# Sorting a graph's edges in 32 steps of 26 columns, with the sums cleared in parts

## The chip, the cores and the metric

The kernel runs on one core of one Trainium2 chip. The metric is the device time of one execution in microseconds (us): the median of three runs of the kernel before is 2950.52 us (2949.51 to 2952.47).

TensorE (PE in the profile) multiplies, VectorE (DVE), ScalarE (ACT) and GpSimd (POOL) work on whole tiles, and SyncE (SP) issues DMAs. DMAs whose addresses come from a table, gathers and scatters, are issued by POOL.

## The reference

A graph layer on 6250 nodes of 256 features and 106250 edges (two directions of 50000 random pairs and one loop per node), then a mixture of six experts, of which each node takes two:

```
deg        = segment_sum(ones, row); denom = maximum(deg, 1)
neigh_sum  = segment_sum(X[col], row)              # X is the layer norm of x
H          = relu(X @ W_root + (neigh_sum / denom) @ W_neigh + b)
gg         = segment_sum(abs(H[row] - H[col])**2, row) / denom
x          = x + tanh(gg)
x          = x + experts(layernorm(x))             # router, top 2 of 6, three layers each
```

Both segment sums go over all edges, so the kernel first brings the edges into the order of their target blocks, on the chip.

## The kernel before, in words

**Stages.** (1) The edges are read, each gets a place by its target's block of 128 nodes (49 blocks), and a table of places is made; this ends some 111 us into the span. (2) The edge sort, which the change touches. (3) The sorted lists are read back and turned into indices (`idx`) and rows within a block (`local`). (4) Pass 1 over the edges: for each of 842 tiles of 128 edges POOL gathers 128 rows of `xn_table`, DVE makes a hot matrix, PE multiplies, DVE adds the product to one block of `acc`. (5) h is made from the sums, (6) pass 2 does the same with `h_table`, (7) the experts.

**The edge sort.** The edges stand in 832 columns (`TW`) of 128. They are taken in 16 chunks (`CC`) of 52 columns (`TH`), and a chunk in steps of `BT` columns; before, `BT` is 13, which is four steps a chunk and 64 in all. In a step `k`, with `c` the chunk and `t` the step in it:

- DVE (`dve_edges`) makes `is_col` (L956: 64 numbers of each column), `hot_lane` (L960: 128 numbers of each), and `hot_col` (L964, two instructions: the first half of it for the columns that ACT leaves over, the second half for all). All are 16-bit products or comparisons of two tiles in SBUF.
- ACT (`act_edges`) makes the first half of `hot_col` for the first `BY_ACT` columns (L776), one instruction for each column.
- PE (`pe_edges`) multiplies `hot_lane` and `hot_col` column by column into one sum per chunk (L692), once all of the step's three parts are there.

`is_col`, `hot_lane` and `hot_col` have two slots each, so step `k` waits until step `k - 2` was used. When a chunk's sum is complete ACT copies its low part (`act_low`, L820), DVE puts low and high together into `lists` (`dve_list`, L1090, with one operand in PSUM), and POOL issues four scatters of the list to `edge_list` in DRAM (L630), each by 128 addresses from `dest`. For the first eight chunks DVE also marks rows (`dve_passed`, L1084), PE sums them (`pe_rows`, L740), and DVE makes the addresses (`dve_rows`, L1098 and L1101, both with an operand in PSUM).

**The product rows beside it.** From step `Z_AT` on, PE makes after each step's products one block of product rows (`pe_z`, L730), and ACT scales it into `z_rows` (`act_z`, L810) one step later. `z_rows` has 8 slots. SP writes four blocks at a time to `xn_table` (`sp_nodes`, L1108); ACT waits for such a write before it overwrites its slots. PE's instructions for the next step stand behind `pe_z`.

**Clearing.** `acc` shares its memory (`big`) with the sort's tiles: columns 0 to `sorting_end` are in use until the sort ends. The rest is cleared while the sort runs, by one DMA that repeats `local`, still zero, 20 times (L534, L536), issued by SP ahead of the writes of product rows. The part below `sorting_end`, 7814 columns, is cleared by DVE (L1175) behind the indices.

What orders the work is the order in which each engine's function issues it; nothing rearranges it. Each engine runs its instructions in that order and waits for semaphores in front of them. The lines of the sort are these:

## Time and profile before

| | |
|---|---|
| median of 3 runs | 2950.52 us |
| span of the profiled execution | 2957.2 us, 32069 instructions |
| PE busy | 2373.3 us (80%) |
| DVE busy | 2010.2 us (68%) |
| ACT busy | 855.2 us (29%) |
| POOL busy | 2030.6 us (69%) |

The profile is of one further execution, whose span from the first to the last instruction is 2957.2 us; the page has no other time of it. Shares over the whole span say little of the sort, which is some 185 us of it. How to read the rows: a scatter or gather on POOL is busy while POOL makes its descriptors; the data land later. Spans of matmuls are modelled, and an instruction of DVE or ACT that follows another closely is shown as starting shortly before the former ends.

### The profile page before, as it was taken

The page shows a single profiled execution, that of the slowest core. Times are in us where ns is not written, and L with a number is a line of the kernel's source. Part 1 is how long each engine was busy: PE and PEld are TensorE (multiplying, and loading weights), DVE is VectorE, ACT ScalarE, POOL GpSimd, SP SyncE. Part 2 cuts the span into 40 slices and gives each one's busy share as a digit, 9 for nine tenths or more (in the row PEclk, how much of TensorE's full clock was granted, in tenths as well). Part 3 has the DMA queues.
Part 4 walks back from the last instruction along what each step waited for, and adds up shares of the span by engine and source line. Part 5 has one row for each costly group of instructions (what it writes and reads, how often), then busy time and mean ns, then how long its engine had stood idle before and what let it go on. Part 6 is the DMA issues. An engine that isn't in the chain of part 4 may idle for free.

```text
span 2957.2 us, 32069 instructions
## 1 busy us (share of the span) xinstructions
PE 2373.3 (80%) x8745; PEld 1336.0 (45%) x8745; DVE 2010.2 (68%) x5189; ACT 855.2 (29%) x2372; POOL 2030.6 (69%) x2062
## 2 busy tenths in 40 slices
PE   6676677777777777773988998889899997899993
PEld 4554444444444444341333333333333333788993
DVE  8997655555555555556777777777777778556654
ACT  7887000000000000003333333333333334455551
POOL 2488777777777777777777777777777772323666
PEclk8597777777777777876999999999999998999997
DMA  3443333333333333335433333333333334333555
GB/s 123 170 98 46 103 106 105 105 105 105 106 105 105 105 105 105 105 105 170 142 105 112 105 105 105 105 105 105 105 105 105 105 105 148 102 122 95 156 152 154
DMA packets 172773, 334.43 MB, mean 113 GB/s; under 512 B 42912, under 2 KB 108428, under 8 KB 172338
## 3 DMA queue, kind: packets, MB, share of 16 engines
q0 software_dynamic: 100176, 249.03, 29.6%
q1 hardware_dynamic: 72418, 83.34, 8.6%
q8 instruction: 72, 1.18, 0.2%
q14 instruction: 107, 0.88, 0.1%
HBM read 281.12 MB, written 41.88 MB: 109 GB/s over the span
## 4 chain that ended last, share of the span: by engine, by line
PE 35%; DVE 19%; DMA 16%; POOL 12%; issue 11%; DVEq 5%; ACT 2%; SPq 0%; POOLq 0%; ACTq 0%
PE ps L1271 22%; DVE big L1312 11%; POOL arena L1237 10%; DMA arena<-xn_table,graph 8%; PE ps L2083 7%; DMA arena<-h_table,graph 4%; DVEq L1281 4%; PE ps L2057 3%; DVE graph L1306 2%; DVE late L1352 1%; ACT big L776 1%; DVE big L964 1%; PE ps L2035 1%; DMA big<-y_table,node 1%; PE ps L1322 1%
## 5 line engine op out<-in xcount | busy, mean ns | idle before, releaser
L1271 PE MATMUL ps<-arena,graph 128*128 128x258 f32 (+3 forms) x3956 | 1706.5, 600 | 398.9 <-DVE graph L1306 388.2
L1271 PEld LDWEIGHTS ps<-arena,graph 128*128 128x128 f32 (+1 forms) x3956 | 773.3, 226 | 1316.0 <-DVE graph L1306 1095.0
L1312 DVE TENSOR_TENSOR big<-ps,big 128x258 f32 (+1 forms) x1978 | 1099.4, 556 | 135.3 <-PE ps L1271 102.0
L1237 POOL DMA_INDIRECT arena<-xn_table,graph x842 | 798.3, 948 | 261.3 <-issue 193.2
L1237 POOL DMA_INDIRECT arena<-h_table,graph x842 | 798.8, 949 | 258.0 <-issue 136.4
L1306 DVE TENSOR_SCALAR graph<-iota,graph 128x128 f32<-128x128 f32 x1684 | 502.1, 298 | 570.6 <-DMA arena<-xn_table,graph 353.9
L1250 ACT ACTIVATE arena<-arena 128x256 f32<-128x256 f32 x842 | 349.4, 416 | 706.6 <-DMA arena<-h_table,graph 706.3
L1368 ACT ACTIVATE node<-late 128x256 f32<-128x256 f32 x49 | 19.7, 413 | 1044.6 <-DVE late L1352 1044.0
L1655 POOL DMA_INDIRECT arena<-xn_table,node x113 | 116.7, 1033 | 211.8 <-PE ps L2035 121.6
L630 POOL DMA_INDIRECT edge_list<-big x64 | 136.2, 2128 | 45.8 <-issue 45.5
L2083 PE MATMUL ps<-arena 128*128 128x128 f32 x904 | 122.2, 279 | 16.3 <-issue 13.6
L776 ACT ACTIVATE big<-arena,big 128x64 f16<-128x64 f16 x512 | 129.7, 363 | 11.7 <-DVE arena L956 11.5
L1704 DVE TENSOR_TENSOR big<-ps,node 128x256 f32<-128x256 f32 x113 | 47.8, 423 | 119.5 <-PE ps L2057 119.2
L1667 POOL DMA_INDIRECT big<-y_table,node x98 | 101.7, 1038 | 33.3 <-issue 23.7
L2083 PE MATMUL ps<-big,arena 128*128 128x128 f32 x904 | 121.8, 279 | 0.0
L2083 PEld LDWEIGHTS ps<-arena 128*128 128x128 f32 x904 | 111.0, 193 | 20.2 <-issue 17.2
L2057 PE MATMUL ps<-node,big 128*128 x452 | 117.8, 384 | 0.8 <-DVE big L1704 0.8
L2083 PEld LDWEIGHTS ps<-big,arena 128*128 128x128 f32 x904 | 112.4, 196 | 0.3 <-issue 0.3
L692 PE MATMUL ps<-big,arena 128*128 128x128 f16 x832 | 69.0, 242 | 46.1 <-ACT big L776 29.2
L1695 DVE COPY arena<-node 128x1028 f32 x113 | 81.8, 725 | 22.2 <-issue 9.3
L692 PEld LDWEIGHTS ps<-big,arena 128*128 128x128 f16 x832 | 58.5, 109 | 67.2 <-issue 53.0
L1974 ACT ACTIVATE big<-ps,arena 128x128 f32<-128x128 f32 x226 | 70.7, 365 | 58.1 <-PE ps L2083 55.7
(319 smaller groups left out, 1596.1 us busy)
## 6 DMA issues: line engine op xcount, KB each, us to landing
y_table<-big SPq DMA_DIRECT2D x55, 256.0 KB, 2.5
arena<-xn_table,graph POOLq DMA_INDIRECT x842, 2.8
arena<-h_table,graph POOLq DMA_INDIRECT x842, 2.7
big<-graph SPq DMA_DIRECT2D x1, 8480.0 KB, 46.5
xn_table<-late SPq DMA_DIRECT2D x12, 512.0 KB
late<-h_table SPq DMA_DIRECT2D x12, 512.0 KB, 4.7
xn_table<-big SPq DMA_DIRECT2D x12, 512.0 KB, 4.6
result<-big SPq DMA_DIRECT2D x12, 512.0 KB
```

Of the source, the lines that this page charges most:

```text
L630: e.indirect_dma_start(out=edge_list[c % 2], out_offset=bass.IndirectOffsetOnAxis(ap=dest[:, c, g:g + 1], axis=0), in_=lists[:, c, g * R8: ...
L692: m = e.matmul(ps[4 + c % 2][:, 0:2 * HI], hot_lane[:, r, u, :], hot_col[:, r, u, :, :].rearrange("p a m -> p (a m)"), start=(t == 0 and u ...
L776: e.activation(hot_col[:, r, u, 0, :], is_col[:, r, u, :], ACT.Copy, scale=code_f[:, t0 + u:t0 + u + 1]).then_inc(s_hcola, 1)
L1237: e.indirect_dma_start(out=row, out_offset=None, in_=table, in_offset=bass.IndirectOffsetOnAxis(ap=idx[:, t:t + 1], axis=0)).then_inc(s_ro ...
L1250: e.activation(rows2[:, sq, :], rows2[:, slot, :], ACT.Square).then_inc(s_sq, 1)
L1271: e.matmul(out_, hot[part, g % HOTS, :], moving, start=True, stop=True).then_inc(s_sum[i], 1)
L1281: _, places = nc.values_load_multi_w_load_instructions(offs[0:1, a:z], engines=[mybir.EngineType.DVE], min_val=0, max_val=(NB - 1) * W2, s ...
L1306: e.tensor_scalar(hot[:, g % HOTS, :], iota[:, :], local[:, t:t + 1], None, ALU.is_equal).then_inc(s_hot[i], 1)
L1312: e.tensor_tensor(block, ps[a % BANKS][:, 0:width], block, ALU.add)._wait_ge(s_sum[i], a + 1).then_inc(s_add[i], 1)
L1655: e.indirect_dma_start(out=xg[:, k % XR, :], out_offset=None, in_=xn_table, in_offset=bass.IndirectOffsetOnAxis(ap=tok[:, k:k + 1], axis=0 ...
L2057: m = e.matmul(ps[3][:, 0:D], h2[:, n % 2, j * P:(j + 1) * P], records_flat[:, bass.ds(place + (W12 + j * D), D)], start=(j == 0), stop=(j ...
L2083: t = e.matmul(bank[:, m * P:(m + 1) * P], wbuf[:, k % WR, at_:at_ + P], moving[:, j * P:(j + 1) * P], start=(j == 0), stop=(j == KD - 1))
```

## The change

A step takes 26 columns, so a chunk has two steps and the sort has 32. `BY_ACT` doubles with it: ACT still makes 16 of 26 columns as it made 8 of 13. `hot_lane` no longer fits into one place and its two slots lie apart, one in `arena` and one in `big`; `hot_col` doubles too. So `sorting_end` grows from 7814 to 11142.

Product rows start at step 3 in place of 6, and two blocks are made a step in place of one. ACT now scales the first of the two after its ninth activation of the next step (`u == BY_ACT // 2`), behind `act_low` where there is one, and the second after its sixteenth. `pe_rows` stands ahead of the waits of its step, `dve_rows` moves to the first step of the next chunk, `dve_list` to the second step, and the variance block `dve_variance` from step 3 to step 1.

The one clearing DMA is cut into 13 parts (`sp_clear`) of one or two repetitions of `local`, each issued by SP behind one write of product rows, 16 repetitions in all. Of the columns below `sorting_end` DVE clears 7002, and ACT the 4140 above them, in nine activations behind its last `act_low`. The semaphore `s_unit` is folded into `s_nrow`.

The diff, without changes of assertions and names:

```diff
-    BT = 13
+    BT = 26
-    Z_AT, ZR = 6, 8
+    Z_AT, ZR, ZS = 3, 8, 2
-    BY_ACT = 8
+    BY_ACT = 16
...
-        hot_lane = arena[:, 0:BT * P].bitcast(F16).rearrange("p (r t m) -> p r t m", r=2, t=BT)
...
+        clear_at = max(codes_at + 2 * NT, codes_at + TW)
+        hot_lane = [a.bitcast(F16).rearrange("p (t m) -> p t m", t=BT)
+                    for a in (arena[:, 0:BT * P // 2], carve_sort(BT * P // 2))]
         sorting_end = at
...
             e.wait_ge(s_pick, NB)
-            times, over = divmod(NB * W2 - sorting_end, NTR)
-            e.dma_start(acc[:, sorting_end:NB * W2 - over].rearrange("p (n w) -> p n w", w=NTR),
-                        local.unsqueeze(1).to_broadcast([P, times, NTR])).then_inc(s_cleared, 16)
-            e.dma_start(acc[:, NB * W2 - over:NB * W2], local[:, 0:over]).then_inc(s_cleared, 16)
+
+        times, over = divmod(NB * W2 - sorting_end, NTR)
+        clear_cut = [times * i // len(z_sets) for i in range(len(z_sets) + 1)]
+        clear_parts = [i for i in range(len(z_sets)) if clear_cut[i + 1] > clear_cut[i]]
+
+        def sp_clear(e, i):
+            n = clear_cut[i + 1] - clear_cut[i]
+            at_ = sorting_end + clear_cut[i] * NTR
+            e.dma_start(acc[:, at_:at_ + n * NTR].rearrange("p (n w) -> p n w", w=NTR),
+                        local.unsqueeze(1).to_broadcast([P, n, NTR])).then_inc(s_cleared, 16)
+            if i == clear_parts[0]:
+                e.dma_start(acc[:, NB * W2 - over:NB * W2], local[:, 0:over]).then_inc(s_cleared, 16)
...
                 c, t = divmod(k, TH // BT)
                 r = k % 2
+                if t == 1 and c < C:
+                    pe_rows(e, c)
                 e.wait_ge(s_hlane, k + 1)
...
                 m.then_inc(s_sorted, 1)
-                if t == 1 and c < C:
-                    pe_rows(e, c)
-                if Z_AT <= k < Z_AT + NB:
-                    pe_z(e, k - Z_AT)
+                for b in z_at(k - Z_AT):
+                    pe_z(e, b)
...
+        def z_at(i):
+
+            return range(ZS * i, min(ZS * i + ZS, NB)) if i >= 0 else range(0)
...
+                made_before = z_at(k - Z_AT - 1)
                 for u in range(BY_ACT):
                     e.activation(hot_col[:, r, u, 0, :], is_col[:, r, u, :], ACT.Copy,
                                  scale=code_f[:, t0 + u:t0 + u + 1]).then_inc(s_hcola, 1)
-                if t == 1 and c:
-                    act_low(e, c - 1)
-                if 0 < k - Z_AT <= NB:
-                    act_z(e, k - Z_AT - 1)
+                    if u == BY_ACT // 2:
+                        if t == 1 and c:
+                            act_low(e, c - 1)
+                        for b in made_before[0:1]:
+                            act_z(e, b)
+                for b in made_before[1:]:
+                    act_z(e, b)
             act_low(e, CC - 1)
+            blank = sorting_end - clear_at
+            for a in range(0, blank, 4 * P):
+                n = min(4 * P, blank - a)
+                e.activation(acc[:, clear_at + a:clear_at + a + n],
+                             ones[:, 0:1].to_broadcast([P, n]), ACT.Copy, scale=0.0).then_inc(s_blank, 1)
...
+                if t == 0 and 0 < c <= C:
+                    dve_rows(e, c - 1)
                 if t == 0 and c < C:
                     dve_passed(e, c)
-                if t == 2 and c:
+                if t == 1 and c:
                     dve_list(e, c - 1)
-                if t == 3 and c < C:
-                    dve_rows(e, c)
-                if k == 3:
+                if k == 1:
                     dve_variance(e)
...
                             z_rows[:, b0 % ZR:b0 % ZR + n, :]).then_inc(s_zout[i % 2], 16)
+                if i in clear_parts:
+                    sp_clear(e, i)
...
-            e.wait_ge(s_cleared, 32)
+            e.wait_ge(s_cleared, 16 * (len(clear_parts) + 1))
...
-            e.memset(acc[:, 0:sorting_end], 0.0).then_inc(s_one, 1)
+            e.memset(acc[:, 0:clear_at], 0.0).then_inc(s_one, 1)
+            e.wait_ge(s_blank, -(-(sorting_end - clear_at) // (4 * P)))
```

In the changed kernel every line below the functions that grew has a higher number: `is_col` is L980, `hot_lane` L984, `hot_col` L988, `dve_list` L1114, ACT's part of `hot_col` L792, `act_low` L844, `act_z` L834.

On DVE, one chunk of the later half, from behind one list (L1090) to the next, stood so before:

```order
L956 TENSOR_TENSOR arena<-graph,arena 128x832
L960 TENSOR_TENSOR arena<-graph,arena 128x1664
L964 TENSOR_TENSOR big<-arena 128x5x64
L964 TENSOR_TENSOR big<-arena 128x13x64
L1090 SCALAR_TENSOR_TENSOR big<-ps,big 128x64
```

The first four rows come four times before the next L1090; the list of a chunk comes behind the third step of the next one. Now the same stretch of DVE reads:

```order
L980 TENSOR_TENSOR arena<-graph,arena 128x1664
L984 TENSOR_TENSOR big<-graph,arena 128x3328
L988 TENSOR_TENSOR big<-arena 128x10x64
L988 TENSOR_TENSOR big<-arena 128x26x64
L1114 SCALAR_TENSOR_TENSOR big<-ps,big 128x64
```

The four come twice between two lists, with twice the columns each, and the list stands behind the second of them.

On ACT, while product rows are made, a step was eight activations and one block of product rows:

```order
L776 ACTIVATE big<-arena,big 128x64 x8
L820 ACTIVATE big<-ps 128x64
L810 ACTIVATE late<-ps,rstd 128x256
L776 ACTIVATE big<-arena,big 128x64 x8
L810 ACTIVATE late<-ps,rstd 128x256
```

Now two steps on ACT read as follows, the step with a chunk's low part first:

```order
L792 ACTIVATE big<-arena,big 128x64 x9
L844 ACTIVATE big<-ps 128x64
L834 ACTIVATE late<-ps,rstd 128x256
L792 ACTIVATE big<-arena,big 128x64 x7
L834 ACTIVATE late<-ps,rstd 128x256
L792 ACTIVATE big<-arena,big 128x64 x9
L834 ACTIVATE late<-ps,rstd 128x256
L792 ACTIVATE big<-arena,big 128x64 x7
L834 ACTIVATE late<-ps,rstd 128x256
```

Of each pair of blocks the first now stands between the ninth and the tenth activation of the step that follows its product, ahead of seven activations that PE needs.

## Rows read from the trace of the kernel before

**Rows 1.** Chain that ended last, in order of time: start us, us, what
```profile
144.54 18.86 DMA xn_table<-late
...
289.94 2.88 DMA edge_list<-big
```

**Rows 2.** The page's costliest groups: line, engine, operation, count | busy, mean ns | idle before
```profile
L1237 POOL DMA_INDIRECT arena<-xn_table,graph x842 | 798.3, 948 | 261.3 <-issue 193.2
```

**Rows 3.** Groups by form, 111.4 to 277 us: count | busy us, mean ns | idle before
```profile
L776 ACT ACTIVATE big<-arena,big 128x64 f16<-128x64 f16 x512 | 129.7, 363 | 11.7 <-DVE arena L956 11.5
L630 POOL DMA_INDIRECT edge_list<-big x57 | 125.4, 2199 | 43.6 <-issue 43.3 <-DMA edge_list<-big 0.3
...
L960 DVE TENSOR_TENSOR arena<-graph,arena 128x1664 f16<-128x1664 f16 x64 | 65.1, 1018 | 1.7 <-PE ps L692 1.4
...
L956 DVE TENSOR_TENSOR arena<-graph,arena 128x832 f16<-128x832 f16 x64 | 37.3, 583 | 5.4 <-ACT big L776 5.4
L964 DVE TENSOR_TENSOR big<-arena 128x832 f16<-128x832 f16 x64 | 37.3, 583 | 0.0
...
L964 DVE TENSOR_TENSOR big<-arena 128x320 f16<-128x320 f16 x64 | 20.3, 317 | 0.0
```

**Rows 4.** Timeline, one step in chunk 8: start us, us, engine, line, what [idle before]
```profile
212.07 2.03 ACT L776 ACTIVATE big<-arena,big 128x64 f16<-128x64 f16 x8
...
213.22 0.58 DVE L956 TENSOR_TENSOR arena<-graph,arena 128x832 f16<-128x832 f16 x1
213.72 1.01 DVE L960 TENSOR_TENSOR arena<-graph,arena 128x1664 f16<-128x1664 f16 x1
213.98 0.48 ACT L810 ACTIVATE late<-ps,rstd 128x256 f32<-128x256 f32 x1
...
214.20 0.92 PE L692 MATMUL ps<-big,arena 128*128 128x128 f16 x13 [0.43 <-ACT big L776]
214.28 1.87 POOL L630 DMA_INDIRECT edge_list<-big  x1 [0.30 <-issue]
214.33 2.04 ACT L776 ACTIVATE big<-arena,big 128x64 f16<-128x64 f16 x8
214.66 0.82 DVE L964 TENSOR_TENSOR big<-arena 128x320 f16<-128x320 f16 x2
...
214.96 1.08 PE L730 MATMUL ps<-late,node 128*128 128x256 f32 x4
```

**Rows 5.** Timeline of DVE and POOL around a long scatter, 195 to 200 us
```profile
195.71 5.41 POOL L630 DMA_INDIRECT edge_list<-big  x1 [0.30 <-issue]
...
195.28 0.58 DVE L956 TENSOR_TENSOR arena<-graph,arena 128x832 f16<-128x832 f16 x1
195.78 1.02 DVE L960 TENSOR_TENSOR arena<-graph,arena 128x1664 f16<-128x1664 f16 x1
...
198.89 0.82 DVE L964 TENSOR_TENSOR big<-arena 128x320 f16<-128x320 f16 x2
...
199.63 0.21 DVE L1090 SCALAR_TENSOR_TENSOR big<-ps,big 128x64 f32<-128x64 f32 x1
```

**Rows 6.** Timeline: the first list, the last two, a scatter then, the first gather
```profile
132.59 0.21 DVE L1090 SCALAR_TENSOR_TENSOR big<-ps,big 128x64 f32<-128x64 f32 x1
...
271.76 0.21 DVE L1090 SCALAR_TENSOR_TENSOR big<-ps,big 128x64 f32<-128x64 f32 x1
...
276.46 0.22 DVE L1090 SCALAR_TENSOR_TENSOR big<-ps,big 128x64 f32<-128x64 f32 x1 [2.31 <-ACT big L820]
276.98 1.54 POOL L630 DMA_INDIRECT edge_list<-big  x1 [0.30 <-issue]
...
296.36 1.03 POOL L1237 DMA_INDIRECT arena<-xn_table,graph  x1 [4.88 <-DVE graph L1193]
```

**Rows 7.** Timeline: ACT behind a write of product rows; DVE's clearing
```profile
163.43 0.47 ACT L810 ACTIVATE late<-ps,rstd 128x256 f32<-128x256 f32 x1 [7.79 <-DMA xn_table<-late]
...
305.88 6.57 DVE L1175 MEMSET big<- 128x7814 f32 x1 [1.81 <-issue]
```

More of the change, by code:

```diff
@@ L129, in gnn_moe_kernel @@
         high, low, lane_of, col_of = (pairs[:, i, :, :] for i in range(4))
-        hot_lane = arena[:, 0:BT * P].bitcast(F16).rearrange("p (r t m) -> p r t m", r=2, t=BT)
         is_col = arena[:, 6 * TW:6 * TW + BT * HI].bitcast(F16).rearrange("p (r t m) -> p r t m", r=2, t=BT)
-        assert BT * P <= 2 * TW and 6 * TW + BT * HI <= SLOTS * W1 + 2 * D
+        assert BT * P // 2 <= 2 * TW and 6 * TW + BT * HI <= SLOTS * W1 + 2 * D
         free = node[:, :, :].rearrange("p b d -> p (b d)")
@@ L232, in gnn_moe_kernel @@
         hot_col = carve_sort(BT * 2 * HI).bitcast(F16).rearrange("p (r t a m) -> p r t a m", r=2, t=BT, a=2)
+        clear_at = max(codes_at + 2 * NT, codes_at + TW)
+        hot_lane = [a.bitcast(F16).rearrange("p (t m) -> p t m", t=BT)
+                    for a in (arena[:, 0:BT * P // 2], carve_sort(BT * P // 2))]
         sorting_end = at
+        assert clear_at < sorting_end
         assert codes_at + 2 * NT <= sorting_end
-        assert PR == ZR and 2 * KD * D + ZR * D <= 6 * KD * D and Z_AT + NB < TW // BT
+        assert PR == ZR and 2 * KD * D + ZR * D <= 6 * KD * D and Z_AT + -(-NB // ZS) < TW // BT
         XAT = -(-taken // D)
@@ L376, in gnn_moe_kernel @@
         s_cnt = sem("counts_summed")
-        s_nrow = sem("totals_and_rows_needed_made")
+        s_nrow = sem("totals_rows_and_units_made")
         s_row0 = sem("totals_carried_first_rows_summed")
@@ L397, in gnn_moe_kernel @@
         s_region = sem("region_constants_made")
-        s_unit = sem("whole_tiles_and_units_made")
         s_unit_sum = sem("region_sums_made")
@@ L406, in gnn_moe_kernel @@
         s_cleared = sem("sums_cleared_by_dma")
+        s_blank = sem("sums_cleared_by_act")
         s_xt = [sem(f"x_columns_in_{i}") for i in range(2)]
@@ L662, in pe_edges @@
             pe_centre(e, 1)
-            e.wait_ge(s_unit, 1)
+            e.wait_ge(s_nrow, 3)
             e.matmul(ps[5][0:NB2, 2:4], below_b[0:NB2, :], block_t[0:NB2, 0:2], start=True, stop=True).then_inc(s_unit_sum, 1)
@@ L691, in pe_edges @@
                 for u in range(BT):
-                    m = e.matmul(ps[4 + c % 2][:, 0:2 * HI], hot_lane[:, r, u, :],
+                    m = e.matmul(ps[4 + c % 2][:, 0:2 * HI], hot_lane[r][:, u, :],
                                  hot_col[:, r, u, :, :].rearrange("p a m -> p (a m)"),
@@ L959, in dve_edges @@
                     e.wait_ge(s_sorted, k - 1)
-                e.tensor_tensor(paired(hot_lane[:, r, :, :]), counted(BT, P), across(lane_of, t0, BT, P),
+                e.tensor_tensor(paired(hot_lane[r]), counted(BT, P), across(lane_of, t0, BT, P),
                                 ALU.is_equal).then_inc(s_hlane, 1)
@@ L1018, in dve_units @@
             e.wait_ge(s_v, v.up())
-            e.scalar_tensor_tensor(units, whole, -float(UNITS), units, ALU.mult, ALU.add).then_inc(s_unit, 1)
+            e.scalar_tensor_tensor(units, whole, -float(UNITS), units, ALU.mult, ALU.add).then_inc(s_nrow, 1)
         def dve_regions(e):
```

## The prediction

> **What bounds the kernel now.** First the page's groups: pass 1 is paced by POOL, 842 gathers of 0.948 us with 261.3 us between them, 0.31 each [rows 2], so it ends when it starts plus a fixed 1060 us, and the start is the first gather at 296.36 [rows 6]. Then the chain in order of time: the sort reaches that gather through the last scatter of a list, which starts at 289.94 and lands 2.88 later [rows 1]. So what the change is worth is how much earlier POOL's 64th scatter starts. The timeline shows that POOL, not DVE, is last there: the last list is made at 276.46 + 0.22 = 276.68, and four scatters of 1.54 + 0.30 [rows 6] would follow it in 7.4 us, the last starting at 282.3, but it starts 7.6 later: POOL is four scatters behind. Two things have to be predicted: when the lists are made, and how far behind them POOL is.
>
> **When the lists are made: DVE's work.** A step of 13 on DVE is 583 + 1018 + 317 + 583 ns [rows 3], less four overlaps of 0.08 (213.22 + 0.58 against 213.72 [rows 4]): 2.18 us. The forms of 832 and 1664 elements give 0.523 ns an element and 0.148 fixed. With 26 columns the four are 1664, 3328, 640 and 1664 elements: 1.018 + 1.888 + 0.483 + 1.018 - 0.32 = 4.08 us against 4.36. That would save 0.27 x 32 = 8.7 us.
>
> **What takes it back: ACT.** ACT's activations stand 0.239 apart (eight in 213.98 - 212.07) and a block of product rows costs 0.35 (214.33 - 213.98), 2.26 a step of 13 [rows 4]; doubled, 4.53. Between them now lies a wait. PE starts its products 0.22 after ACT's last activation slot, is through 13 in 0.76 and makes a block in 1.08 [rows 4]. With 26 products the first block is ready 0.22 + 1.52 + 1.08 = 2.82 after that slot. ACT first does the second block of the pair before (0.35), then nine activations (2.15), and stands at 2.50; so it waits 0.32 for the block, 0.4 with the semaphore, with seven activations that PE needs queued behind it. A step of ACT is 4.93 and a chunk 9.86. Before, ACT took product rows after all eight, and they were ready. I bound the wait by 0 (chunk 9.1) and 0.5 (10.1).
>
> DVE's chunk would be 2 x 4.08 + list 0.13 = 8.3, and 9.4 in the first eight chunks with their extra 1.1. ACT is therefore the bound in chunks 2 to 13, all those with product rows. Before, the lists from chunk 6 (199.63 [rows 5]) to 14 (271.76 [rows 6]) stood 9.02 apart. Here the change loses 0.84 a chunk.
>
> It gains earlier. The one clearing DMA in front of the writes of product rows made a write last 18.86 us [rows 1], ACT waited 7.79 for its slots [rows 7] and DVE 5.4 for ACT [rows 3]. Each write now has only one or two repetitions of 20 ahead of it, and I take that stall as gone; its bounds are 0 and 5.4.
>
> The sum: the first list comes behind four steps of 4.08 in place of seven of 2.18, 1.1 later than 132.8 [rows 6], at 133.9. The next takes 10.8 (first blocks at a slow PE), then eleven at 9.86 put list 12 at 253.2; list 13 at 262.8 has one step without blocks; list 14 after 8.3 at 271.1, 0.9 before the 271.97 of before [rows 6]. The last list needs only three steps' tail: 26 products in 1.6 and ACT's and DVE's last two instructions put it at 274.3, against 276.68. So out of 8.7 + 5.4 expected, 0.9 to 2.4 us are left.
>
> **How far POOL is behind.** An undisturbed scatter takes 1.54 [rows 6], but most take 1.87 and some 5.41. In rows 4 a scatter starts at 214.28 and ends at 216.15, 1.41 behind the end of L960 (213.72 + 1.01 = 214.73). So it asks for something 1.54 - 1.41 = 0.13 after its start, and gets it when the DVE instruction in progress ends. In rows 5 one starts at 195.71 and asks at 195.84, between the start of L960 (195.78) and the end of L956 (195.86), when two DVE instructions overlap. It ends at 201.12, again 1.41 behind the end of a DVE instruction, L964 at 199.71; but seven earlier ends went by, and what followed this one is L1090, which reads one operand in PSUM. I read: a request that falls into the 0.08 in which two instructions with two SBUF operands overlap waits until one of the other kind follows.
>
> Here the Trainium skill is to be weighed ("SBUF — State Buffer", Who interferes with whom): a DVE instruction with two SBUF inputs contends with what GpSimd reads from SBUF, and it adds, as inferred, that tensor_tensor does not hold up the making of descriptors. By the first half scatters wait; by the second none would. The rows show the wait.
>
> From one release to the next request is 1.41 + 0.30 + 0.13 = 1.84. With 26 columns, behind the release at the end of the short `hot_col` (its next instruction, `hot_col` part two, has started 0.08 before) the following `hot_lane` starts 1.79 later and `is_col` ends 1.87 later: a request there falls into the overlap, and the scatter waits for the list, 4.7 us in all. In the first eight chunks `dve_passed` and `dve_rows` lie between and POOL makes four a chunk. From chunk 9 on there are two steady patterns, of four a chunk and of three with a 4.7 among them; which one depends on tenths of a microsecond at chunk 8. In the pattern of four, POOL is one behind at list 14, and the last scatter ends at 271.1 + 9 x 1.84 = 287.7 against 289.94 + 1.54 = 291.5: 3.8 earlier.
>
> **What costs nothing.** ACT's nine clearing activations: 512 elements each, bounded by 0.2 and 1 us, so 2 to 9 us from 274.3 on, before DVE's own clearing starts some 14 us behind the last scatter (305.88 against 291.5 [rows 1, 7]). DVE clears 7002 in place of 7814 columns in 6.57 x 7002 / 7814 = 5.89, 0.7 less; POOL runs ahead of it, sixteen gathers deep (16 x 1.26 = 20 us from 296.36, while DVE is through at 312.45), so this is worth 0, at most 0.7. Nothing of the clearing parts is near the end: the last is issued at block 48, some 15 us before the last list.
>
> **The forecast.** 2950.5 - 3.8 = 2946.7 us. The differences are made in the profiled execution, of 2957.2 span, 6.7 above the median; I subtract them from the median.
>
> **The rivals.**
>
> - *B, three scatters a chunk.* The request lands in the overlap once in every chunk from 9 to 15, and POOL is seven behind at list 14: 15 scatters remain, 271 + 15 x 1.84 = 298.7, 7.2 us later than before: 2957.7. For it speaks that the overlap is hit by 0.03 to 0.05 on either side, as it was repeatedly in rows 5; against it, that the pattern must be entered. It decides when the chunk's period is right for it: a few tenths more or less of ACT's wait.
> - *C, DVE stays the bound.* ACT's wait is hidden or smaller than I think. Lists: 133.9 + 7 x 9.4 + 7 x 8.3 = 257.8, and the last scatter at 257.8 + 8 to 12 x 1.84, 272.5 to 280: 11 to 19 us earlier, 2932 to 2940. Against it stands the order on ACT.
> - *D, scatters are not held by DVE at all.* Then only the lists count: 274.3 + 4 x 1.84 = 281.7, 9.8 earlier, 2940.7. The second half of the skill's rule would give this; against it stand the 1.87 and 5.41 of rows 4 and 5.
> - *E, most requests are missed.* Long instructions leave few ends: one or two scatters a chunk from chunk 9, 20 behind: 271 + 28 x 1.84 = 322.5, 31 later, 2981. Against it: in the trace a request in the middle of an instruction was served at its end.
>
> **How the numbers follow.** Forecast (A) 0.43, B 0.35, C 0.10, D 0.07, E 0.05. A's own range is 2941 to 2949, for the bounds of ACT's wait (12 chunks x 0.1) and two scatters more or less. The limit of what can be told from no change is 0.2%, 5.9 us: A is mostly within it, a quarter beyond; B is beyond it in most of its width (2953 to 2961). So faster 0.28, same 0.34, slower 0.38. A range of 2937 to 2962 leaves out E and part of C, about 0.12.
>
> **What would show it.** DVE's four instructions at 1.02, 1.89, 0.48 and 1.02. ACT waiting about 0.4 before the first block of each pair, 24 times, on PE's L730; lists 9.8 to 9.9 apart up to chunk 13 and no wait of 7.8 for a write. The last two lists near 271 and 274.3. Scatters of about 4.7 from chunk 9 on, one a chunk (B) or none (A). The start of pass 1 moved by the same amount as the end of the last scatter, and pass 1 and everything behind it as long as before. Wrong would be: lists closer than 9.5 (C), scatters of 1.54 amid DVE's work (D), or a change of pass 1's own length.

## The result, and the profile after

The changed kernel takes 2957.07 us (median of 12 runs) against 2951.99 for the kernel before in the same comparison (12 runs): a ratio of 1.0017, 95% interval 1.0010 to 1.0024, so 5 us slower (3 to 7 by the interval). I had forecast 2946.7 us, with an estimate of 3.8 us less.

The lists of the changed kernel come as forecast. In the timeline (start us, us, engine, line, what, [idle before and what ended it]) the first, the last two, the last scatter and the first gather are:

```profile
132.91 0.22 DVE L1114 SCALAR_TENSOR_TENSOR big<-ps,big 128x64 f32<-128x64 f32 x1
...
269.74 0.21 DVE L1114 SCALAR_TENSOR_TENSOR big<-ps,big 128x64 f32<-128x64 f32 x1
272.84 0.23 DVE L1114 SCALAR_TENSOR_TENSOR big<-ps,big 128x64 f32<-128x64 f32 x1 [2.89 <-ACT big L844]
294.21 1.54 POOL L641 DMA_INDIRECT edge_list<-big  x1 [0.30 <-issue]
300.42 1.02 POOL L1264 DMA_INDIRECT arena<-xn_table,graph  x1 [4.66 <-DVE graph L1220]
```

Against [rows 6] the last list is 3.6 us earlier and the last scatter ends 4.3 us later (295.75 against 291.48); the first gather moved by the same, 296.36 to 300.42. Pass 1 itself kept its length: 842 gathers of 947 ns with 261.2 us between them, against [rows 2].

```profile
L1264 POOL DMA_INDIRECT arena<-xn_table,graph x842 | 797.0, 947 | 261.2 <-issue 195.6
```

The profiled execution of after has a span of 2956.1, 1.1 less than that of before, although its pass 1 starts 4.1 later; 1.1 of that comes back in pass 1, 2.8 in the stage behind it and 1.3 in the last part. The 4.1 by which pass 1 starts later lie within the interval of the medians, which are 5.1 apart, and single executions of one kernel differ by up to 8.6 us. So below I read the start of pass 1 in each trace first, and the ratio second.

Where did POOL lose it? These rows group the scatters that lie in 134 to 199 us (the first eight chunks or so) and in 199 to 264: count | busy us, mean ns | idle before. First the kernel before, then after:

```profile
L630 POOL DMA_INDIRECT edge_list<-big x22 | 58.6, 2665 | 33.0 <-issue 33.0
L630 POOL DMA_INDIRECT edge_list<-big x30 | 61.5, 2048 | 9.1 <-issue 9.1
```

```profile
L641 POOL DMA_INDIRECT edge_list<-big x15 | 61.4, 4095 | 29.5 <-issue 28.3 <-DVE big L1125 0.9 <-DVE big L1114 0.3
L641 POOL DMA_INDIRECT edge_list<-big x34 | 58.3, 1714 | 10.4 <-issue 9.8 <-DMA edge_list<-big 0.6
```

In the first stretch after makes 15 scatters where before made 22, in the second it gains four back. It is three behind: 3 x 1.84 = 5.5 us, measured 4.3. The same count settles the prediction's sum: when list 14 was made, at 269.95, 14 scatters had still to start where I had put 9, and 269.95 + 14 x 1.84 = 295.7 is the measured end, 295.75. The timeline of one early chunk of after shows how a chunk comes to hold only two scatters:

```profile
175.91 1.42 DVE L988 TENSOR_TENSOR big<-arena 128x640 f16<-128x640 f16 x2
177.25 0.16 DVE L1122 SCALAR_TENSOR_TENSOR big<-ps,rownum 128x8 f32<-128x8 f32 x1
177.44 0.17 DVE L1125 TENSOR_TENSOR big<-big,ps 128x8 uint32<-128x8 f32 x1
177.53 0.95 DVE L1108 TENSOR_TENSOR big<-big,small 98x1536 f16<-98x1536 f16 x1
177.71 6.25 POOL L641 DMA_INDIRECT edge_list<-big  x1 [0.30 <-issue]
178.39 1.02 DVE L980 TENSOR_TENSOR arena<-graph,arena 128x1664 f16<-128x1664 f16 x1
179.33 1.89 DVE L984 TENSOR_TENSOR big<-graph,arena 128x3328 f16<-128x3328 f16 x1
181.13 1.43 DVE L988 TENSOR_TENSOR big<-arena 128x640 f16<-128x640 f16 x2
182.89 0.22 DVE L1114 SCALAR_TENSOR_TENSOR big<-ps,big 128x64 f32<-128x64 f32 x1 [0.33 <-ACT big L844]
183.03 1.02 DVE L980 TENSOR_TENSOR arena<-graph,arena 128x1664 f16<-128x1664 f16 x1
183.96 1.88 DVE L984 TENSOR_TENSOR arena<-graph,arena 128x3328 f16<-128x3328 f16 x1
184.27 2.99 POOL L641 DMA_INDIRECT edge_list<-big  x1 [0.30 <-issue]
```

The scatter at 177.71 begins 0.18 into L1108, the instruction of `dve_passed`, and ends at 183.96, 1.41 behind the end of L988 at 182.56, where DVE runs out of work. It let four earlier ends go by. The next begins 0.31 into L984, is served at L984's end, and 6.25 + 0.30 + 2.99 + 0.30 = 9.84 is the chunk: the pattern reproduces itself.

### The profile page after: what moved, and what is told of

Its sections match the earlier page's. It is cut to its first block, busy times and chain, and to the rows that moved or that the text cites. A ratio compares the mean times of both kernels' runs of the same rounds, so it can differ in the third digit from the quotient of the medians.

```text
span 2956.1 us, 31867 instructions
## 1 busy us (share of the span) xinstructions
PE 2370.3 (80%) x8745; PEld 1345.1 (46%) x8745; DVE 2001.4 (68%) x5061; ACT 859.0 (29%) x2381; POOL 2034.4 (69%) x2062
## 4 chain that ended last, share of the span: by engine, by line
PE 36%; DVE 14%; DMA 13%; POOL 12%; issue 9%; DVEq 5%; ACT 1%; POOLq 0%; ACTq 0%
PE ps L1298 23%; POOL arena L1264 11%; DVE big L1339 10%; DMA arena<-xn_table,graph 7%; PE ps L2110 7%; DMA arena<-h_table,graph 4%; DVEq L1308 4%; PE ps L2084 3%; DVE graph L1333 2%; DVE late L1379 1%; PE ps L2062 1%; PE ps L1349 1%; DMA big<-y_table,node 1%; ACT arena L1277 1%; PE ps L2133 1%
## 5 line engine op out<-in xcount | busy, mean ns | idle before, releaser
L1298 PEld LDWEIGHTS ps<-arena,graph 128*128 128x128 f32 (+1 forms) x3956 | 781.5, 228 | 1301.6 <-DVE graph L1333 1057.0
L1264 POOL DMA_INDIRECT arena<-xn_table,graph x842 | 797.0, 947 | 261.2 <-issue 195.6
L641 POOL DMA_INDIRECT edge_list<-big x64 | 142.6, 2228 | 44.4 <-issue 42.6
L792 ACT ACTIVATE big<-arena,big 128x64 f16<-128x64 f16 x512 | 127.7, 337 | 10.4 <-DVE arena L980 10.4
L2001 ACT ACTIVATE big<-ps,arena 128x128 f32<-128x128 f32 x226 | 70.5, 364 | 60.2 <-PE ps L2110 57.4
L2084 PEld LDWEIGHTS ps<-node,big 128*128 128x128 f32 x452 | 77.8, 192 | 7.1 <-issue 1.2
L2009 ACT ACTIVATE big<-ps,arena 128x128 f32<-128x128 f32 x226 | 70.7, 365 | 28.9 <-PE ps L2110 28.7
```

What stands on the lines that cost most here:

```text
L641: e.indirect_dma_start(out=edge_list[c % 2], out_offset=bass.IndirectOffsetOnAxis(ap=dest[:, c, g:g + 1], axis=0), in_=lists[:, c, g * R8: ...
L792: e.activation(hot_col[:, r, u, 0, :], is_col[:, r, u, :], ACT.Copy, scale=code_f[:, t0 + u:t0 + u + 1]).then_inc(s_hcola, 1)
L1264: e.indirect_dma_start(out=row, out_offset=None, in_=table, in_offset=bass.IndirectOffsetOnAxis(ap=idx[:, t:t + 1], axis=0)).then_inc(s_ro ...
L1298: e.matmul(out_, hot[part, g % HOTS, :], moving, start=True, stop=True).then_inc(s_sum[i], 1)
L2084: m = e.matmul(ps[3][:, 0:D], h2[:, n % 2, j * P:(j + 1) * P], records_flat[:, bass.ds(place + (W12 + j * D), D)], start=(j == 0), stop=(j ...
```

## The experiments

After the comparison I held **theory T**: the instruction of `dve_passed` starts a stretch in which a waiting scatter is passed over, until DVE runs something else than a tensor_tensor with two SBUF operands or stands idle. Its rivals: **R**, the rule of my prediction (only the 0.08 us overlap of two instructions does it); **Q**, transfers slow the scatters, not DVE; and **L**, the time follows the lists.

The runs were made in four groups, each with the kernel before on the same chip: first a_swap, a_tiny, b_tiny and b_parts; second a_act, a_swap_act, b_parts_tiny and a_probe; third a_rows and a_best; fourth a_probe2 and a_one. In the first, second and fourth group the kernel before took 3357.8, 3318.6 and 3326.9 us (pass 1 lasts 1199 to 1213 us in the traces of these groups, against 1053 to 1055 in before, after, a_rows and a_best; why isn't shown), in the third 2954.1. The sort is the same in all to 1 or 2 us at its first list, so the times of its steps are compared across groups, the totals only within one. "a" kernels are made from the changed kernel, "b" kernels from the one before; all times in us.

| kernel | first list | last list | last scatter ends | first gather | ratio to before (95%) |
|---|---|---|---|---|---|
| before | 132.8 | 276.7 | 291.5 | 296.4 | |
| after | 133.1 | 273.1 | 295.8 | 300.4 | 1.0017 (1.0010 to 1.0024) |
| a_swap | 133.3 | 273.7 | 284.6 | 290.1 | 0.9981 (0.9966 to 0.9996) |
| a_tiny | 134.0 | 274.8 | 285.6 | 290.6 | 0.9994 (0.9977 to 1.0010) |
| b_tiny | 133.1 | 276.9 | 288.0 | 292.8 | 0.9995 (0.9979 to 1.0011) |
| b_parts | 132.1 | 268.8 | 290.9 | 296.0 | 1.0004 (0.9990 to 1.0018) |
| a_act | 134.3 | 266.7 | 302.9 | 307.6 | 1.0030 (1.0016 to 1.0043) |
| a_swap_act | 132.9 | 264.6 | 277.8 | 282.9 | 0.9974 (0.9961 to 0.9987) |
| b_parts_tiny | 133.5 | 269.5 | 281.2 | 286.2 | 0.9961 (0.9945 to 0.9976) |
| a_probe | 133.6 | 273.1 | 319.5 | 324.6 | one run |
| a_rows | 133.9 | 274.7 | 285.6 | 290.5 | 0.9981 (0.9972 to 0.9990) |
| a_best | 132.7 | 261.0 | 275.0 | 279.9 | 0.9961 (0.9947 to 0.9974) |
| a_probe2 | 134.0 | 274.6 | 325.5 | 330.5 | one run |
| a_one | 134.4 | 274.7 | 298.0 | 302.9 | 1.0004 (0.9992 to 1.0017) |

The times follow the first gather in the main, not to the microsecond. In a_swap_act and a_best it starts 13.5 and 16.5 earlier than in before while the medians differ by 8.3 and 12.9, and in a_one it starts 6.6 later, 0.20%, where the interval ends at 0.17%. Where the rest goes isn't shown.

**a_swap: the instruction of dve_passed in front of one that reads PSUM.**

```diff
-                if t == 0 and 0 < c <= C:
-                    dve_rows(e, c - 1)
                 if t == 0 and c < C:
+                    if c:
+                        e.wait_ge(s_jumped, c)
                     dve_passed(e, c)
+                if t == 0 and 0 < c <= C:
+                    dve_rows(e, c - 1)
```

> The changed kernel with dve_passed(c) put ahead of dve_rows(c - 1) in the first step of a chunk (two calls swapped). In its trace the scatters of the first eight chunks last 6.25 and 2.9-3.0 us, two a chunk, and each of 6.25 begins inside dve_passed (L1108). Theory T (the instruction of dve_passed starts a stretch in which a waiting scatter is passed over, until DVE runs something other than a tensor_tensor with two SBUF operands or stands idle): the next instruction is now L1122, which reads PSUM, so nothing is passed over; no scatter lasts over 3.3 us, POOL makes four a chunk, the last one ends at 280 to 284 in place of 295.75, and the time is 2957 - 12 to 15 = 2942 to 2945. Theory R (the rule of the prediction: only a request in the 0.08 us in which two instructions overlap is passed over, dve_passed is nothing special): the swap alters only phases; scatters over 4 us stay, the last scatter within 4 us of 295.75, time 2953 to 2960. Theory Q (the scatters are slow for the transfers of the product rows and the clearing parts, not for DVE): nothing changes, 2957.

Only the first scatter of all is over 3.4 us (3.57), none after it over 2.8; the last ends at 284.6, 11.2 earlier than in after, with the lists where they were. T holds, R and Q fall. The end is 0.6 beyond what I gave, and the gain in time, 0.19%, is less than 12 to 15 us; it fits the 6.3 by which the first gather is earlier than in before.

**a_tiny and b_tiny: a memset of one column behind it.**

```diff
                             starts_two[:, :, c, :].unsqueeze(2).to_broadcast(every), ALU.is_ge).then_inc(s_passed, 1)
+            e.memset(blip[:, c:c + 1], 0.0)
```

> The changed kernel with a memset of one column right behind the instruction of dve_passed, eight in all. Theory T, if any instruction without two SBUF operands ends the stretch: the scatters of 6.25 us, which begin 0.2 us into L1108, are served at about its end and last 2.2 to 2.4; the last scatter ends at 280 to 285, time 2943 to 2946. Theory T, if only a read of PSUM or an idle DVE ends it: nothing changes, 2957. Theory R: a request inside a single instruction should never have waited beyond it, so R says nothing of why these last 6.25 and expects no change from a memset that costs 0.1 us x 8: 2957 to 2958. Theory Q: 2957.

> The kernel before with the same memset right behind the instruction of dve_passed (L1084). There the long scatters (5.41 us) ask 0.4 us after the end of L1084, where L956 and L960 overlap, so behind the memset. Theory T: the memset has ended the stretch, and they are served at the end of L960, 2.3 to 2.7 us; POOL, four scatters behind at the end, keeps up; the last scatter ends at 282 to 286 in place of 291.5, time 2952 - 6 to 9 = 2943 to 2946. Theory R: the overlap of L956 and L960 is still there 0.4 us behind the memset, the scatters stay at 5.4, time 2951 to 2953.

The memset ends the stretch: a_tiny has its last scatter at 285.6, as a_swap. b_tiny is the sharper test. There the scatters that answer to the one of [rows 5] keep the place where R saw the cause (asking at 195.94 + 0.13 = 196.07, in the overlap of L957 and L961), yet they last 1.6 in place of 5.4:

```profile
194.64 0.95 DVE L1085 TENSOR_TENSOR big<-big,small 98x1536 f16<-98x1536 f16 x1
195.52 0.58 DVE L957 TENSOR_TENSOR arena<-graph,arena 128x832 f16<-128x832 f16 x1
195.54 0.06 DVE L1088 MEMSET blip<- 128x1 f32 x1
195.94 1.58 POOL L631 DMA_INDIRECT edge_list<-big  x1 [0.30 <-issue]
196.03 1.02 DVE L961 TENSOR_TENSOR arena<-graph,arena 128x1664 f16<-128x1664 f16 x1
```

The last scatter ends at 288.0, not at 282 to 286: a part of what was won is lost again at the first scatter of a chunk, which now waits for its list and then takes 2.83 to 2.86 in four chunks. Neither ratio is told from 1 by its interval.

**b_parts: only the clearing in parts, in the kernel before.** Edit: the one DMA of the sums goes, `sp_clear(e, i)` is called behind each write of product rows, as in the change.

> The kernel before, 64 steps of 13, with only the clearing of the sums in parts behind the writes of product rows (no clearing by ScalarE). All theories: ACT's wait of 7.79 us for a write goes and DVE's wait of 5.4 with it, so the last list is made at 271 to 272 in place of 276.7. Theories T and R: POOL makes three scatters a chunk in the first eight chunks (5.41 + 2.00 + 1.65 and three gaps of 0.30) and used the 5.4 us of DVE's standstill to catch up; without it POOL is about seven behind and the last scatter ends at 290 to 293 as before: time 2950 to 2954, no gain. Theory Q (transfers slow the scatters): the last scatter ends 5 us earlier too, 2946 to 2948.

ACT's wait of 7.79 is gone and the last list is made at 268.8, 7.9 earlier (more than the 5.4 I gave). The last scatter ends 0.6 earlier. T's "no gain" is what came: POOL paces the sort. L and Q fall.

**a_act and a_swap_act: the order on ScalarE.**

```diff
-                    if u == BY_ACT // 2:
-                        if t == 1 and c:
-                            act_low(e, c - 1)
-                        for b in made_before[0:1]:
-                            act_z(e, b)
-                for b in made_before[1:]:
+                    if u == BY_ACT // 2 and t == 1 and c:
+                        act_low(e, c - 1)
+                for b in made_before:
                     act_z(e, b)
```

> The changed kernel with both blocks of product rows made by ScalarE behind all sixteen activations of a step, in place of the first behind nine. It isolates one term of the prediction, the wait of 0.4 us for the first block. If that wait is what makes a chunk 9.86: a step of ACT is 4.53, chunks are 9.1 to 9.4 (9.4 is DVE's in the first eight), the last list is made at 264 to 267 in place of 273.1. Theory T (scatters are passed over behind dve_passed): POOL still makes two a chunk in the first eight, so it is 16 or more behind when they end at about 200; from there 1.84 to 2.1 each, the last one ends at 293 to 299 and nothing is gained: time within 0.1% of the changed kernel. Theory L (the lists are what the time hangs on): 6 to 9 us less.

> Both edits on the changed kernel: dve_passed ahead of dve_rows, and both blocks of product rows behind the sixteen activations. With the passing over gone POOL follows the lists, so what the order on ACT gives now shows: last list at 264 to 267 (with the swap alone 273.7), last scatter ends at 273 to 278 (284.6), first gather of pass 1 at 278 to 283 (290.1; 296.4 in the kernel before): 13 to 18 us, 0.4 to 0.6% below the kernel before. If the chunk of 9.86 has another cause than ACT's wait: 284 and 290 again, 0.2% below.

In after ACT did wait for the first block of each pair; in the timeline of a late step:

```profile
224.87 2.25 ACT L792 ACTIVATE big<-arena,big 128x64 f16<-128x64 f16 x9
226.23 1.94 PE L745 MATMUL ps<-late,node 128*128 128x256 f32 x8
227.41 0.47 ACT L834 ACTIVATE late<-ps,rstd 128x256 f32<-128x256 f32 x1 [0.29 <-PE ps L745]
227.78 1.76 ACT L792 ACTIVATE big<-arena,big 128x64 f16<-128x64 f16 x7
```

With the two blocks behind all sixteen the lists stand 9.4 apart in the first eight chunks and 9.15 behind them, in place of 9.86, so that term is confirmed: 0.7 a chunk where DVE isn't the bound. But a_act, whose last list is 6.4 earlier, has its last scatter 7.1 later (302.9, beyond the 299 I allowed) and is 0.3% slower than before: in shorter chunks POOL still makes two scatters, of 4.9 and 3.9. Those of 4.9 begin behind `dve_passed` (L1105 here) as T has it. Those of 3.9, one in each of six chunks, T doesn't explain: the list (L1111, which reads PSUM) stands between, and still the end of L981 at 174.72 goes by. From the timeline:

```profile
171.77 0.22 DVE L1111 SCALAR_TENSOR_TENSOR big<-ps,big 128x64 f32<-128x64 f32 x1
...
172.84 1.88 DVE L981 TENSOR_TENSOR arena<-graph,arena 128x3328 f16<-128x3328 f16 x1
...
173.57 3.90 POOL L641 DMA_INDIRECT edge_list<-big  x1 [0.30 <-issue]
```

Served at that end it would have lasted 174.72 + 1.41 - 173.57 = 2.56, so the six cost some 8 us by this estimate, about what a_act is late. In a_swap_act, where dve_passed is followed by a read of PSUM, no scatter lets an end go by but the first of all. The same edit on top of a_swap makes the last scatter 6.8 us earlier. In these kernels an earlier list is worth something only where scatters aren't passed over.

**b_parts_tiny: the two edits on before together.**

> The kernel before (64 steps of 13) with the clearing in parts and the memset behind dve_passed. Apart they moved the first gather of pass 1 from 296.4 to 296.0 and 292.8. Theory T: the parts bring the last list to 269 to 270 and were worth nothing because POOL was seven scatters behind; with the memset it makes four a chunk, so the last scatter ends at 277 to 281 and the first gather starts at 282 to 286: 10 to 14 us, 0.3 to 0.5%, below the kernel before, more than the sum of the two alone (4). If the two simply add: 292.4.

10.2 us for the first gather and 0.39%, where the two alone gave 0.4 and 3.6: they don't add. The 64 steps of 13 with two small edits are no slower in time than the steps of 26 with theirs (a_swap_act), though their first gather is 3.3 later.

**a_probe: what is it in that instruction?**

```diff
+                if t == 0 and 8 <= c < 14:
+                    n = (NB2, P, 96)[(c - 8) // 2]
+                    spare = passed.rearrange("p j (t m) -> p (j t) m", m=P)
+                    e.tensor_tensor(paired(spare)[0:n], counted(12, P)[0:n], across(lane_of, t0, 12, P)[0:n],
+                                    ALU.is_equal)
```

> What is it in dve_passed? The changed kernel with one more tensor_tensor in the first step of chunks 8 to 13, where the real dve_passed no longer runs and POOL still has scatters waiting: 1536 f16 elements like L1108, with the operands of hot_lane (the counting row and the lanes), on 98 rows in chunks 8 and 9, 128 rows in 10 and 11, 96 rows in 12 and 13. Its result is used nowhere. Theory T-rows (an instruction on fewer than 128 rows starts the stretch in which scatters are passed over; L1108 has 98): scatters of 4 to 6.3 us in chunks 8, 9, 12, 13, none in 10 and 11. Theory T-place (any further instruction between hot_col and the next is_col): in all six. Theory T-form (something of L1108's own operands): in none, scatters 1.54 to 2.3 as in the changed kernel.

Four of the six added instructions, those of chunks 9 to 12, and the scatters that followed (from the timelines of DVE and of POOL; those in chunks 8 and 13 lasted 6.25 and 5.97):

```profile
206.61 0.95 DVE L997 TENSOR_TENSOR big<-graph,arena 98x1536 f16<-98x1536 f16 x1
207.07 5.98 POOL L641 DMA_INDIRECT edge_list<-big  x1 [0.30 <-issue]
...
216.58 0.95 DVE L997 TENSOR_TENSOR big<-graph,arena 128x1536 f16<-128x1536 f16 x1
217.04 1.90 POOL L641 DMA_INDIRECT edge_list<-big  x1 [0.30 <-issue]
...
226.34 0.95 DVE L997 TENSOR_TENSOR big<-graph,arena 128x1536 f16<-128x1536 f16 x1
226.80 1.90 POOL L641 DMA_INDIRECT edge_list<-big  x1 [0.30 <-issue]
...
236.20 0.95 DVE L997 TENSOR_TENSOR big<-graph,arena 96x1536 f16<-96x1536 f16 x1
236.66 5.97 POOL L641 DMA_INDIRECT edge_list<-big  x1 [0.30 <-issue]
```

Each of these four begins 0.46 into the added instruction. On 98 and 96 rows it lasts 5.97 to 5.98, on 128 rows 1.90: operands, length, place and phase are the same, the rows differ. Theory T-rows holds.

**a_rows: the same instruction on all 128 rows.**

```diff
-            every = [NB2, 3, GG * P // 2, 2]
-            e.tensor_tensor(passed[0:NB2, :, :].rearrange("p j (r q) -> p j r q", q=2),
-                            count_h[0:NB2, :].rearrange("p (r q) -> p r q", q=2).unsqueeze(1).to_broadcast(every),
-                            starts_two[:, :, c, :].unsqueeze(2).to_broadcast(every), ALU.is_ge).then_inc(s_passed, 1)
+            every = [P, 3, GG * P // 2, 2]
+            starts_all = small[:, 0:3 * C].bitcast(F16).rearrange("p (j c q) -> p j c q", j=3, q=2)
+            e.tensor_tensor(passed.rearrange("p j (r q) -> p j r q", q=2),
+                            count_h.rearrange("p (r q) -> p r q", q=2).unsqueeze(1).to_broadcast(every),
+                            starts_all[:, :, c, :].unsqueeze(2).to_broadcast(every), ALU.is_ge).then_inc(s_passed, 1)
```

> The changed kernel with the instruction of dve_passed on all 128 rows in place of 98 (the 30 added rows are used nowhere; one memset of 24 columns ahead of the sort gives them a value). Nothing moves. Theory T-rows (what starts the passing over is that the instruction has fewer than 128 rows): the first scatter of a chunk, which begins 0.2 us into L1108 or its like, is served at that instruction's end and lasts 2.2 to 2.4 in place of 6.25; no scatter over 3.3; last scatter ends at 280 to 286, first gather at 286 to 291 (300.4 in the changed kernel, 296.4 before), time 0.1 to 0.3% below before. Theory T-form (the operands of L1108): two a chunk as in the changed kernel, 300 for the first gather, 0.1 to 0.2% above before.

The timeline of the stretch that was shown of after:

```profile
177.79 0.16 DVE L1128 TENSOR_TENSOR big<-big,ps 128x8 uint32<-128x8 f32 x1
177.88 0.95 DVE L1111 TENSOR_TENSOR big<-big,small 128x1536 f16<-128x1536 f16 x1
178.06 2.17 POOL L641 DMA_INDIRECT edge_list<-big  x1 [0.30 <-issue]
178.74 1.02 DVE L980 TENSOR_TENSOR arena<-graph,arena 128x1664 f16<-128x1664 f16 x1
179.68 1.88 DVE L984 TENSOR_TENSOR big<-graph,arena 128x3328 f16<-128x3328 f16 x1
180.54 2.43 POOL L641 DMA_INDIRECT edge_list<-big  x1 [0.30 <-issue]
```

A scatter again begins 0.18 into the instruction. It is served at its end (178.83 + 1.41 = 180.24) and lasts 2.17, not 6.25. In 134 to 199 us POOL makes 26 scatters instead of 15, of 2.2 us instead of 4.1:

```profile
L641 POOL DMA_INDIRECT edge_list<-big x26 | 57.7, 2219 | 32.7 <-issue 32.7
```

The last scatter ends 10.2 earlier than in after with the last list 1.6 later, and the time is 0.19% under the kernel before. Nothing was moved within the sort, so this is the cause by itself.

**a_probe2: which instructions on fewer rows?** The added instruction is a tensor_tensor on 64 rows, a copy of 98 rows (one SBUF operand) and an f32 tensor_tensor on 98 rows.

```diff
+                if t == 0 and 10 <= c < 12:
+                    e.tensor_copy(passed[0:NB2, :, :],
+                                  count_h[0:NB2, :].unsqueeze(1).to_broadcast([NB2, 3, GG * P]))
```

> Which instructions on fewer than 128 rows do it? As the probe before, with another added instruction: in chunks 8 and 9 the tensor_tensor on 64 rows (f16, two SBUF operands), in 10 and 11 a tensor_copy of 1536 f16 elements on 98 rows (one SBUF operand), in 12 and 13 a tensor_tensor of 768 f32 elements on 98 rows. Their results are used nowhere. Theory T-rows as it stands (any instruction on fewer than 128 rows): scatters of 4 to 6.3 us in all six chunks. Theory T-rows-tt (only a tensor_tensor): in 8, 9, 12, 13. Theory T-rows-f16 (only an f16 tensor_tensor): in 8 and 9 alone. The small instructions on 98 rows and one column, all ahead of the sort, leave this open.

All do: the scatters behind the six added instructions last 6.24, 5.97, 5.96, 5.97, 5.97 and 5.98. The copy at 217.03 and the f32 instruction at 236.74 are each followed by a long scatter (timelines):

```profile
217.03 0.94 DVE L999 COPY big<-big 98x1536 f16<-98x1536 f16 x1
217.50 5.96 POOL L641 DMA_INDIRECT edge_list<-big  x1 [0.30 <-issue]
...
236.74 0.94 DVE L1003 TENSOR_TENSOR big<-ones,ident 98x768 f32<-98x768 f32 x1
237.20 5.97 POOL L641 DMA_INDIRECT edge_list<-big  x1 [0.30 <-issue]
```

**a_one: the changed kernel with the sums cleared by one DMA up front.**

> The changed kernel with the sums cleared by the one DMA ahead of the writes of product rows, as before the change. The prediction gave the parts 5.4 us of earlier lists. Theory T: the stall of ScalarE for the write comes back (5 to 8 us, last list at 278 to 281 in place of 273.1), but while DVE stands still POOL makes the scatters that it was behind with, at 1.84 each; the last scatter ends at 295 to 298 and the first gather within 2 us of 300.4: the parts are worth 0 to 2 us in the changed kernel, time within 0.1% of it. Theory L (the lists count): first gather at 306, 0.2% more than the changed kernel.

My expectation failed in its first half: no stall came back. Between 125 and 200 us ACT waits for no DMA at all; this row has its waits for blocks (us in total, times, longest):

```profile
ACT late L837 <- PE ps L748: 4.0, 11, 1.6
```

So in the changed kernel it isn't the parts that took the stall away. Two things differ from before: the DMA clears 6784 KB, not 8480, since the second `hot_lane` buffer lies in the sums and ScalarE clears what it covers, and the first write is issued at 146.59, 2.05 later than in [rows 1]. Which of them does it wasn't tried. The first gather is 2.5 later than in after and the first list 1.3 later, so the parts are worth about 1 us there.

**a_best: what the runs point to.** a_rows, the order of a_act, and `BY_ACT = 14`.

> The version that the runs point to: the changed kernel with dve_passed on 128 rows, both blocks of product rows behind the activations, and 14 activations a step on ScalarE in place of 16 (DVE's third instruction then has 12 columns, 768 elements). A step of ACT: 14 x 0.239 + 0.70 = 4.05; a step of DVE: 4.08 + 128 x 0.523 ns = 4.15, so DVE is the bound, chunks 9.5 in the first eight and 8.4 to 8.5 behind them: last list at 258 to 261. POOL needs 7.4 a chunk at least and 8.5 if one or two requests are held, so it is one to four behind: last scatter ends at 268 to 274, first gather at 273 to 279, 17 to 23 us before the kernel before's 296.4: 0.5 to 0.7% less time. If POOL stays at the 9.1 a chunk that it had with both edits before (2.90 + 1.97 + 1.54 + 1.54 and gaps): last scatter 277, first gather 283, 0.4%.

2941.22 us against 2954.1 for the kernel before on the same chip, 12.9 us less, and the first gather at 279.9. Lists are made as expected (the last at 261.0, behind the first eight chunks 8.5 apart), but both the end of the last scatter and the first gather lie 1 us beyond my range: POOL, at 2.16 + 1.54 + 2.03 + 1.54 and four gaps of 0.30, takes just the chunk of 8.5 and catches nothing up; seven scatters start behind the last list. The timeline of one such chunk:

```profile
211.62 1.01 DVE L977 TENSOR_TENSOR arena<-graph,arena 128x1664 f16<-128x1664 f16 x1
212.02 2.03 POOL L641 DMA_INDIRECT edge_list<-big  x1 [0.30 <-issue]
212.56 1.88 DVE L981 TENSOR_TENSOR big<-graph,arena 128x3328 f16<-128x3328 f16 x1
214.35 1.54 POOL L641 DMA_INDIRECT edge_list<-big  x1 [0.30 <-issue]
...
216.20 2.16 POOL L641 DMA_INDIRECT edge_list<-big  x1 [0.30 <-issue]
```

## Why the prediction was wrong

- **The bound: right.** The start of pass 1 hangs on the 64th scatter, not on the last list, and pass 1 shifted whole. In every run the first gather starts 4.7 to 5.5 behind the end of the last scatter; a_act, with earlier lists and a later end, shows most plainly that the lists don't decide.
- **DVE's and ACT's work: right.** I gave chunks of 9.86, the first list at 133.9 and the last two at 271.1 and 274.3; they came 9.86 apart, at 133.1, 269.9 and 273.1. ACT's wait is 0.29 in one step and 0.18 behind `act_low` in the other; the order that caused it costs 0.7 a chunk behind the first eight (a_act), near my 0.76, and 0.4 in them, where DVE is the bound.
- **The stall gone: right as a fact, wrong as a gain.** It was worth 7.9 us of lists in b_parts and nothing in time. In the changed kernel it would have gone without the parts (a_one).
- **"A request that falls into the 0.08 in which two instructions with two SBUF operands overlap waits until one of the other kind follows": this step failed.** I had it from one scatter, [rows 5], and it fitted the others. The cause stood 1.3 us ahead of that scatter, just above the stretch I read:

```profile
194.41 0.95 DVE L1084 TENSOR_TENSOR big<-big,small 98x1536 f16<-98x1536 f16 x1
```

  Seven scatters of before let an end go by; but for the very first, all begin 1.3 to 1.8 us behind a start of L1084, and none comes after chunk 8, where L1084 stops. b_tiny kept the overlap and lost the wait; a_probe and a_rows changed the rows alone and the wait came and went with them.
- **"In the first eight chunks ... POOL makes four a chunk": failed with it.** I took `dve_passed` for one more instruction that gives POOL openings. It shut POOL out, and in longer steps it did so for longer: 6.25 us in place of 5.41, and, since the step repeats in phase, in every chunk. POOL made two a chunk, once three, so that at list 14 the sum's "9 x 1.84" was in fact 14 x 1.84. a_rows puts the price at 10 us.
- **Behind chunk 9**, where I feared scatters of 4.7 us (rival B), there are none: POOL runs at 1.71 a scatter and catches up. B's 2957.7 is close to the measured time, and its 15 remaining scatters to the 14, but by luck: its mechanism never happened. I also had no term for a request that is served at once: behind chunk 9 the scatters that begin together with a DVE instruction take 1.54.
- **The clearing by ScalarE** costs nothing, as said; DVE's own went from 6.57 to 5.89.

## What to carry to other kernels

Before a change is priced by the lists an engine makes, find the engine that runs behind them, and count how many of its items lie in each stretch: 15 against 22 told where the loss was made. Where GpSimd issues indirect DMAs beside a busy VectorE, look what stands ahead of each long one; an instruction on fewer than 128 rows among full ones is suspect, and giving it all rows, or a memset of one column behind it, costs 0.1 us or nothing and made the last scatter end 3.5 to 10 us earlier here. One explained scatter isn't a rule: tabulate all that are long, with what they have in common.

## What the runs showed of the hardware

- A DVE instruction on 64, 96 or 98 rows (tensor_tensor in f16 and f32, copy) starts a stretch in which POOL's next indirect DMA isn't served at the ends of the instructions that follow; it ends when DVE idles, or with a memset of one column, or with an instruction that reads PSUM. In such a stretch even a scatter that begins together with an instruction is held: the second scatter of all, begun together with L984, lasts 4.65 in after and 1.55 in a_rows. Beside instructions on 128 rows alone most scatters wait to the end of the instruction in progress (2.17 in a_rows) or, where they begin together with it, not at all (1.54). Why the rows matter the traces don't show.
- It isn't the only way to be passed over. The first scatter of every kernel lasts 3.0 to 5.0 us, also in a_rows and a_best, and in b_tiny and b_parts_tiny the first of a chunk, after a pause of POOL of 1.1 us or more, takes 2.85 and lets L961's end go by (L969's in the other), with no instruction on fewer rows since the memset. The pause alone isn't it: scatters behind pauses of 2.3 us in a_rows take 1.61. In a_act six scatters of 3.9 let L981's end go by although L1111 had read PSUM since. That stays open.
- The prediction weighed the Trainium skill's "SBUF — State Buffer", Who interferes with whom. Its inference that tensor_tensor does not hold up the making of descriptors disagrees with these traces: a scatter of 1.54 us took 1.87 to 6.25 beside it. What it says of contention between a two-input instruction and what GpSimd reads from SBUF fits these waits; which access of the scatter waits no trace shows. The copy with one SBUF operand on 98 rows was followed by a scatter of 5.96 too.
